# Cross-attention and mixture of experts on one core: four fp32 slots for the exps, their low parts on two engines, and one slot for a key head's result

## The reference

```python
# attention, with ctx as keys and values
q  = layernorm(x)
scores  = einsum('bkgsd,bktd->bkgst', q_heads, ctx_heads) / sqrt(32)
weights = softmax(scores, axis=-1)
x = x + einsum('bkgst,bktd->bkgsd', weights, ctx_heads)
# mixture of experts: 8 experts, 2 per row, inner width 704
xf = layernorm(x)
top2, idx = top_k(xf @ router_w.T, 2);  w = softmax(top2)
y1 = xf[expert rows] @ w1[e].T;  gate, up = split(y1, 2)
x = x + sum over the 2 experts of (silu(gate) * up) @ w2[e].T * w
```

## Time and profile before

| | |
|---|---|
| median of 3 runs | 10446.44 us (10442.45 to 10451.76) |
| profiled execution | 10468.8 us |
| its span, first to last instruction | 10467.1 us |
| TensorE busy | 8700.9 us, 83% |
| VectorE busy | 5420.6 us, 52% |
| ScalarE busy | 4553.4 us, 44% |
| GpSimd busy | 4817.5 us, 46% |
| GpSimd line L1170, low parts of the exps | 2048 of 1180 ns, 2412.4 us |
| ScalarE lines L944, L945 | 2048 each of 688 and 682 ns |

### The profile page before, as it was taken

The page is one execution under the profiler, slowest core; times in us unless marked ns, Lnnn a source line. Parts: engine busy times, 40 slices in busy tenths (PEclk is TensorE's granted clock), DMA queues, the critical chain, the costliest instruction groups (busy, mean ns, idle before and its releaser), DMA issues. The chain is left out here.

```text
span 10467.1 us, 213020 instructions
## 1 busy us (share of the span) xinstructions
PE 8700.9 (83%) x73448; PEld 4862.2 (46%) x73448; DVE 5420.6 (52%) x10971; ACT 4553.4 (44%) x6962; POOL 4817.5 (46%) x6069
## 2 busy tenths in 40 slices
PE   4455558988888988888988888988888989989989
PEld 3233334544444544444544444544444545544457
DVE  7766665555555555555555555555555555322212
ACT  4456554544444544444544444544444544300001
POOL 0166665555555555555555555555555555311111
PEclk7656569999999999999999999999999999999999
DMA  9742124444444444444444444444444444544444
GB/s 368 274 161 93 50 81 126 133 120 122 121 130 124 132 118 124 121 129 125 132 119 124 121 128 126 132 120 122 121 130 124 133 120 124 145 153 161 167 158 168
DMA packets 455377, 1433.81 MB, mean 137 GB/s; under 512 B 90088, under 2 KB 110568, under 8 KB 454128
## 3 DMA queue, kind: packets, MB, share of 16 engines
q1 hardware_dynamic: 360240, 1132.12, 32.4%
q0 software_dynamic: 94016, 287.65, 11.7%
HBM read 1034.41 MB, written 408.21 MB: 138 GB/s over the span
## 5 line engine op out<-in xcount | busy, mean ns | idle before, releaser
L1170 POOL TENSOR_TENSOR a_pl<-a_p,a_ph 128x512 f16<-128x512 f32 x2048 | 2412.4, 1180 | 2803.7 <-ACT a_ph L945 2245.0
L860 PE MATMUL e_y<-e_xt,e_w 128*128 128x512 f16 x14520 | 3640.7, 390 | 0.6 <-DMA e_w<-w_parts 0.6
L944 ACT ACTIVATE a_p<-a_sc,a_escale 128x512 f32<-128x512 f32 x2048 | 1408.7, 688 | 3610.7 <-PE a_sc L702 2249.6
L1343 DVE TENSOR_REDUCE a_nmax<-a_mx 128x2 f32<-128x512 f32 x2048 | 1406.3, 688 | 1582.7 <-PE a_mx L719 1570.3
L860 PEld LDWEIGHTS e_y<-e_xt,e_w 128*128 128x128 f16 x14520 | 1401.8, 99 | 1444.0 <-issue 141.0
L881 PE MATMUL e_y<-e_w,e_yt 128*128 128x512 f16 x7480 | 1863.8, 379 | 41.1 <-DVE e_yt L1499 41.1
L702 PE MATMUL a_sc<-a_qs,a_ks 128*128 128x512 f16 x2048 | 855.5, 418 | 1234.0 <-ACT a_ph L945 1211.7
L945 ACT ACTIVATE a_ph<-a_sc,a_escale 128x512 f16<-128x512 f32 x2048 | 1396.6, 682 | 0.0
L881 PEld LDWEIGHTS e_y<-e_w,e_yt 128*128 128x128 f16 x7480 | 694.5, 97 | 698.2 <-issue 65.0
L719 PE MATMUL a_mx<-a_ks,a_qs 96*128 96x256 f16 x4096 | 870.6, 297 | 120.3 <-DVE a_nmax L1343 114.0
L702 PEld LDWEIGHTS a_sc<-a_qs,a_ks 128*128 128x128 f16 x2048 | 204.0, 100 | 1585.9 <-ACT a_ph L945 731.3
(11 more groups left out here) (235 smaller groups left out, 11214.9 us busy)
## 6 DMA issues: line engine op xcount, KB each, us to landing
e_w<-w_parts SPq DMA_DIRECT2D x935, 512.0 KB, 3.4
f_w<-w_parts SPq DMA_DIRECT2D x153, 512.0 KB, 5.0
w_parts<-w_parts SPq DMA_DIRECT2D x136, 512.0 KB, 4.9
h_w<-w_parts SPq DMA_DIRECT2D x136, 512.0 KB, 6.1
a_x<-in_x SPq DMA_DIRECT2D x64, 1024.0 KB, 6.2
a_xres<-in_x SPq DMA_DIRECT2D x64, 1024.0 KB, 7.8
out<-a_xres SPq DMA_DIRECT2D x64, 1024.0 KB, 7.1
xn_parts<-a_xhl SPq DMA_DIRECT2D x64, 1024.0 KB, 9.9
```

The lines of the kernel that those rows point to most:

```text
L860: last = pe.matmul(Y[:, bank, :], w1r[:, t % RING, h, pw, :], xT[:, px, h, :], start=r == 0, stop=r == 3 * HT - 1)
L944: act.activation(PF[:, q % 2, :], SC[:, :], ACT.Exp, scale=escale[:, sp_:sp_ + 1])
L1170: pool.tensor_tensor(PL[:, kv % 2, q // 2, q % 2, :], PF[:, q % 2, :], PH[:, kv % 2, q // 2, q % 2, :], ALU.subtract).then_inc(n["p_low"], 1)
L1343: dve.reduce_max(nmax[:, half, kv * G + 2 * gp:kv * G + 2 * gp + 2], MX[:, q % 2, :, :], AX.X, negate=True).then_inc(n["maxed"], 1)
```

## The change

It has three parts. `PF` gets four slots, one for each q. The low parts of q = 2 and 3 are made by VectorE, behind `max_rows_out` and behind `max_out(3)` of the same k, and counted in a semaphore of their own, `p_low2`; GpSimd keeps q = 0 and 1. `exps` of q waits for the low part of the same q of the key head before, on the semaphore of the engine that makes it; `values` waits for both. `att` keeps one slot in place of two, so `o_out` of unit u waits for GpSimd's adds of unit u-1.

```diff
-        PF = sb("a_p", [P, 2, 2 * S], F32)
+        PF = sb("a_p", [P, 4, 2 * S], F32)
-        att = sb("a_att", [P, 2, 2, G, D], F32)
+        att = sb("a_att", [P, 2, G, D], F32)
+        p_low2 = sem("a_p_low2")
...
             def values(i, k, par):
-                pe.wait_ge(n["p_low"], b * 32 + (4 * kv + 4))
+                pe.wait_ge(n["p_low"], b * 16 + (2 * kv + 2))
+                pe.wait_ge(p_low2, b * 16 + (2 * kv + 2))
...
             def exps(i, k, par, q):
-                at_least(act, n["p_low"], b * 32 + (4 * kv + q - 1))
-                act.activation(PF[:, q % 2, :], SC[:, :], ACT.Exp, scale=escale[:, sp_:sp_ + 1])
+                at_least(act, n["p_low"] if q < 2 else p_low2, b * 16 + (2 * kv + q % 2 - 1))
+                act.activation(PF[:, q, :], SC[:, :], ACT.Exp, scale=escale[:, sp_:sp_ + 1])
...
             # GpSimd, attended
-                        pool.tensor_tensor(to, att[:, u % 2, c, :, :].rearrange("p g d -> p (g d)"), to, ALU.add)\
+                        pool.tensor_tensor(to, att[:, c, :, :].rearrange("p g d -> p (g d)"), to, ALU.add)\
             # GpSimd, low_p
-                    pool.tensor_tensor(PL[:, kv % 2, q // 2, q % 2, :], PF[:, q % 2, :],
+                    pool.tensor_tensor(PL[:, kv % 2, q // 2, q % 2, :], PF[:, q, :],
             # GpSimd, iteration
                     attended(i, k, par)
-                    low_p(i, k, 2)
...
-                    low_p(i, k, 3)
...
+            # VectorE
+            def low_p(i, k, q):
+                b, kv = scu(i, k)
+                if on(b):
+                    dve.wait_ge(n["exps"], b * 32 + (4 * kv + q + 1))
+                    dve.tensor_tensor(PL[:, kv % 2, q // 2, q % 2, :], PF[:, q, :],
+                                       PH[:, kv % 2, q // 2, q % 2, :], ALU.subtract).then_inc(p_low2, 1)
...
             def o_out(i, k, par):
-                    at_least(dve, n["x1_done"], b * 16 + 2 * (u - 1))
+                    at_least(dve, n["x1_done"], b * 16 + 2 * u)
-                        out=att[:, u % 2, :, :, :], in0=PV[:, :, :, 0:D], scalar=vscale[:, vp:vp + 1],
+                        out=att[:, :, :, :], in0=PV[:, :, :, 0:D], scalar=vscale[:, vp:vp + 1],
...
             # VectorE, iteration
                     max_out(i, k, 2)
                     max_rows_out(i, k)
+                    low_p(i, k, 2)
                     experts(i, 8 * k + 5, par, fused)
...
                     max_out(i, k, 3)
+                    low_p(i, k, 3)
                     if k == 7 and on(i):
                         scale_values(i, par)
```

## The result

The changed kernel takes **10094.4 us** (median of 4 runs, 10091.9 to 10099.3) against 10448.5 for the kernel before, a ratio of 0.966 (95% interval 0.965 to 0.968). The forecast was 10110. Its profiled execution has a span of 10091.3 us.

What follows compares the result with a forecast made beforehand. TensorE bounds the kernel, with a hole each step from GpSimd's chain around the all-reduce. 5.8 us a step, 51 times (296 us), plus 44 us early gives 340 us: 10446.4 becomes 10110 us, range 10010 to 10320.

Steps and rivals of the forecast that it cites:

- the single event: GpSimd's chain around the all-reduce delays low part 1 of k = 0, stopping TensorE; at most 19.9 us a step.
- Four slots, 6.3 us: Beside experts, TensorE stops at score 2 of k = 1 instead of score 0, gaining 6.3 us a step.
- the sum: Gain over the whole kernel: 296 us beside experts plus 44 us ahead of them, 340 us in total.
- VectorE's low parts, 0.5 us a step: Low parts 2 and 3 on VectorE cost 0.2 us on GpSimd's chain and 0.3 us off it.
- One att slot, 0: VectorE's wait at o_out of k = 1 is covered by TensorE's idle: cost 0, up to 3 us a step uncovered.
- The early stage, 44 us: Ahead of the experts, to 1500 us, the same event: 4 us gained in each of 11 steps.
- the small stall: TensorE's 1.96 us idle behind low part 0 of k = 0 disappears; no extra gain from it.
- the new line: VectorE's added low-part instruction takes 0.7 to 1.1 us.
- A: Idle pieces inside GpSimd's chain shorten too, hole shrinks by 10 us or more: about 9880 us; chance 0.06.
- B: VectorE's debt of 3 us in k = 1 reaches TensorE, half the gain: about 10300 us; chance 0.17.
- C: VectorE's in-order queue becomes the limit, its low parts delaying TensorE: slower, about 10610 us; chance 0.09.
- D: Another condition holds TensorE at score 0 of k = 1, hole unmoved: about 10430 us; chance 0.06.

Runs made afterwards that it cites:

- e4: Kernel before with the all-reduce of the context's maximum replaced by a GpSimd copy, output not the reference's: 9495.6 us, ratio 0.911.
- e1: Kernel before with four fp32 slots and one att slot, all low parts staying on GpSimd: 10081.0 us, ratio 0.968.
- e3: Kernel before with one att slot alone, still two fp32 slots: 10422.0 us, ratio 1.000.
- e12: e1 run again beside the changed kernel on the same chip: 10089.3 us, ratio 0.967.
- e11: The changed kernel run again, beside e12 on the same chip: 10084.8 us, ratio 0.967.
- e7: Changed kernel with GpSimd's low part 1 and add to x moved ahead of the all-reduce in k = 0: 9706.2 us, ratio 0.932.
- e9: e1 with low part 1 and the add to x moved ahead of the all-reduce in k = 0: 10008.0 us, ratio 0.960.
- e2: Changed kernel with two fp32 slots in place of four, low parts 2 and 3 still on VectorE: 10431.2 us, ratio 1.001.

## Why the prediction was right

- **What bounds the kernel, and the single event.** Shown. Leaving out the all-reduce gives 923 us (e4). The hole per step was put at 19.9 us at most; 15.8 us go with the all-reduce, and 2.9 us more are a difference between tail steps and full ones.
- **Four slots, 6.3 us.** The mechanism is shown: the release is fixed by GpSimd, two scores' worth of work moves ahead of it, TensorE now stops at score 2 of k = 1, and the slots without VectorE's share (e1) have the gain. The clock stays low behind the idle as before. The size is a little smaller than the term: e1's steps are 5.8 us shorter than those of e3 on the same chip. (Against the one profile of the kernel before, e1 has 6.6 and the changed kernel 6.4, but that execution was 20 us above its median.) With the early steps, the sum had 321 + 44 = 365 us for the slots alone; e1 gained 337 us and e12 344.
- **VectorE's low parts, 0.5 us a step.** Wrong in size: 0 (-4 us in all, beside e12), where the sum had 25 us of cost. An instruction takes 741 ns, not 1121. Of the 1024 in the changed kernel's trace, 757 overlap no GpSimd instruction other than DMA issues, and none of these takes over 0.69 us; of the other 267, 142 take over 0.8 us. Placed like this, few of them meet. On the chain the first wide instruction of `enter` fell from 0.63 to 0.18 us, as said, which pays most of the 0.6 us ahead of it.
- **One att slot, 0.** Shown for two fp32 slots (e3, ratio 1.000). With four, VectorE's 12.85 us at `o_out` stand under the hole in the step shown; there the att slot was not tried apart.
- **The early stage, 44 us.** Up to the first all-reduce beside experts e1 gains 45 us on e3, and the changed kernel 41 on the kernel before. A typical early step gains less than the 4 us assumed in the changed kernel, 2.8, and the steps at both ends of the stage more. VectorE's share costs 9 us there (e11 beside e12), which the sum had left out.
- **The sum, and some luck.** 340 us predicted, 354 measured by the medians (348 when run again, e11). That it is so near is in part luck: the term for the slots was 20 to 30 us too large and the cost of VectorE's low parts 25 us too large, and the two cancel. The profiled executions differ by 376 us, 41 + 322 + 13 where the sum had 44 + 296, mostly because that of the kernel before was 20 above its median. Of the 13 us behind the last all-reduce the sum counts one hole, as the last of its 51; some 7 us it had not counted.
- **The signs.** The all-reduces come every 136.3 us (137 said), the small stall is gone, the new line takes 741 ns (700 to 1100 said), and VectorE idles at the reciprocal. TensorE's wait at the scores is 9.1 us a step where 11 or 12 were said: that holds for every second step alone, since in the others part of the idle is the older wait for the maxima. The chance of a clock kept up by the shorter idle did not come true.
- **The rivals.** A (the idle pieces shorten) didn't happen: over the 47 all-reduces past 2000 us the two pieces are 16.6 us together before and 16.7 after. (The lower end of the forecast's own range, 7.7 x 51 + 88 = 481 us, should have read 9965, not 9980.) B and C (VectorE's debt) didn't either, by e3 and the pair e11, e12. D fell with e1.

## What to carry to other kernels

When waits come once or twice a period and are long, look for the one event behind them and ask what stands behind it in its engine's order; moving low part 1 and the add to x ahead of it (e7) brought more than the buffers did, though only with VectorE's share beside it: without, the same move brought 73 us (e9 against e1). More buffers only shift such a hole by the work that they let pass, which can be computed ahead of time from the distance of the instructions. A relief of the engine that holds the event is worth nothing as long as the chain is on it (e2), and may be worth 3% once the order is changed (e9 against e7), so parts should be judged again after each step.

## What the runs showed of the hardware

- GpSimd's all-reduce has an idle piece on either side. In the kernel before, the one ahead is 5.8 to 6.9 us in the early steps from 593 to 1334 us and 6.0 to 9.7 past 2000 us, the one behind 6.8 to 7.4 and 7.9 to 10.4. Replacing the all-reduce by a copy takes both away (e4), though the indirect DMA behind it stays. What they are was not tried further.
- A VectorE subtraction with two SBUF inputs of 128x512 took 0.67 to 0.70 us when GpSimd was idle, and 1.19 at 5042.90 in the changed kernel, while GpSimd ran its low part from 5042.39 to 5043.55. The Trainium skill (GPSIMD Engine Reference, Key points) has GpSimd share its SBUF interfaces with VectorE; by that rule the trace agrees, and the mean of 741 ns and the count above say that with this placement few of the 1024 are hit.
- TensorE's granted clock falls in idles of 12 us as it did in those of 15: in the changed kernel's timeline it is 0.50 from 5030 to 5035, and the six expert products behind the idle that ends at 5037.88 took 2.77 us, those before it 1.46. Behind the shorter idles of the other kind of step, 3.76 us to 4880.73 and 6.28 us to 4902.06, six such products took 2.73 and 2.77 us too, at a granted clock of 0.50.
